# Quantised weights through DRAM with transposing loads, and other buffers and gather order ahead of the rounds

## What is computed

```python
xn = layernorm(x)
x = x + gnn(xn, edge_index) + mix(xn)          # graph attention, and linear attention without softmax
x = x + ffn(layernorm(x))

# gnn: rms-normalised x @ W_down, then xl = x @ Wl, xr = x @ Wr (4 heads of 64)
msg = xl[src] + xr[dst]
e = sum(leaky_relu(msg) * att);  p = exp(e - max_per_dst)
out = segment_sum(p / denom * xl[src]) @ W_up

# mix: q, k, v = projections of xn;  out = ((q k^T) * SCALE) v;  out @ Wo + bo

# ffn: every linear works on values rounded to 4-bit blocks of 16 with an 8-bit scale
gate = fq(x) @ fq(gate_w).T;  up = fq(x) @ fq(up_w).T
y = fq(silu(gate) * up) @ fq(down_w).T
```

## Time and profile before

| | us |
|---|---|
| median of three runs | 1021.11 |
| lowest and highest | 1013.91, 1021.95 |
| the profiled execution, in all | 1011.44 |
| its span | 1009.6 |
| mean granted PE clock in it | 0.954 of full |

### The profile page before, as it was taken

One profiled execution on the slowest core, in us unless ns is written; L12 is line 12 of the kernel. 1 busy time (PEld: TensorE's weight loads), 2 busy tenths in 40 slices (PEclk: granted clock), 3 DMA queues, 4 the chain that ended last, 5 costly groups with the idle time before them and its releaser, 6 DMA issues.

```text
span 1009.6 us, 9845 instructions
## 1 busy us (share of the span) xinstructions
PE 908.6 (90%) x2890; PEld 438.5 (43%) x2890; DVE 874.8 (87%) x1032; ACT 557.7 (55%) x1942; POOL 452.8 (45%) x502
## 2 busy tenths in 40 slices
PE   4999999999989999996998999979999779998655
PEld 3776454644344444442443444434444334443222
DVE  7997989976979999999988899788897698776996
ACT  2223133314787787778979898888793441222220
POOL 5210353215767777677776778777640000000000
PEclk9999999999979999998999999989999988999767
DMA  8204343524553533554335533338622000000012
GB/s 284 84 2 121 118 119 82 177 67 137 182 90 97 175 97 92 169 178 115 96 98 168 158 111 101 94 94 307 221 58 73 1 0 1 21 22 21 21 42 79
DMA packets 59460, 105.28 MB, mean 104 GB/s; under 512 B 24631, under 2 KB 32468, under 8 KB 59130
## 3 DMA queue, kind: packets, MB, share of 16 engines
q0 software_dynamic: 18560, 50.70, 19.0%
q1 hardware_dynamic: 40842, 53.92, 15.6%
HBM read 92.30 MB, written 12.45 MB: 104 GB/s over the span
## 4 chain that ended last, share of the span: by engine, by line
DVE 33%; PE 26%; ACT 23%; issue 14%; DMA 2%; POOL 1%; another core or an unknown queue 1%; DVEq 0%; ACTq 0%; POOLq 0%
ACT round_mem L1070 17%; PE acc L663 13%; PE acc L840 6%; DVE turned L1549 5%; DVE acc_sb L1416 5%; DVE z L1551 5%; DVE turned L1408 3%; ACT pz L1057 3%; PE acc L843 2%; DVE round_mem L1169 1%; PE acc L873 1%; PE turned L891 1%; DVE round_mem L1170 1%; DVE round_mem L1168 1%
## 5 line engine op out<-in xcount | busy, mean ns | idle before, releaser
L507 POOL DMA_INDIRECT round_mem<-msg_table,idx x352 | 337.0, 957 | 177.1 <-issue 79.3
L1070 ACT ACTIVATE round_mem<-round_mem,pz 128x65 f32<-128x65 f32 x1408 | 361.6, 398 | 49.0 <-issue 28.1
L663 PE MATMUL acc<-wslot,big_a 128*128 128x512 f32 x512 | 227.9, 606 | 13.1 <-remote 7.5
L663 PEld LDWEIGHTS acc<-wslot,big_a 128*128 128x128 f32 x512 | 98.8, 195 | 138.2 <-issue 129.8
L1416 DVE TENSOR_REDUCE acc_sb<-round_mem 128x260 f32<-128x1820 f32 (+1 forms) x62 | 121.6, 1961 | 42.9 <-ACT round_mem L1070 20.7
L663 PE MATMUL acc<-big_b,wslot 128*128 128x512 f32 x256 | 112.6, 602 | 6.2 <-remote 6.2
L663 PE MATMUL acc<-wslot,big_b 128*128 128x512 f32 x256 | 110.0, 592 | 0.0
L1408 DVE TENSOR_TENSOR turned<-round_mem,turned 128x1560 f32<-128x1560 f32 (+1 forms) x62 | 105.4, 1700 | 4.8 <-issue 2.0
L1551 DVE TENSOR_REDUCE z<-turned 128x24 f32<-128x1560 f32 (+1 forms) x62 | 105.1, 1695 | 2.1
L1549 DVE SCALAR_TENSOR_TENSOR turned<-turned,att_sb 128x1536 f32<-128x1536 f32 (+1 forms) x62 | 103.5, 1670 | 0.0
L1057 ACT ACTIVATE pz<-z 128x7 f32<-128x7 f32 (+1 forms) x248 | 56.8, 295 | 55.2 <-issue 40.6
(11 more groups left out here) (201 smaller groups left out, 1058.6 us busy)
## 6 DMA issues: line engine op xcount, KB each, us to landing
big_b<-in_x SPq DMA_DIRECT2D x18, 512.0 KB
round_mem<-msg_table,idx POOLq DMA_INDIRECT x352
out_x<-big_b SPq DMA_DIRECT2D x9, 512.0 KB
wslot<-in_wv_t SPq DMA_DIRECT2D x2, 2048.0 KB
wslot<-in_wk_t SPq DMA_DIRECT2D x2, 2048.0 KB
wslot<-in_wo_t SPq DMA_DIRECT2D x2, 2048.0 KB
wslot<-in_wq SPq DMA_DIRECT2D x2, 2048.0 KB
wslot<-in_gate_w SPq DMA_DIRECT2D x1, 2048.0 KB
```

The source lines that it names most:

```text
L507: pool.indirect_dma_start(xg[g % 4][:, j, :], None, msg_table, bass.IndirectOffsetOnAxis(idx[:, c, j0 + j:j0 + j + 1], 0)).then_inc(xg_in[ ...
L663: mm = nc.tensor.matmul(o(acc[:, n % 4, :]), a, b, start=first, stop=last)
L1070: ins = nc.scalar.activation(to[:, :, j], xg[g % 4][:, j, h * HR + 1:(h + 1) * HR], ACT.Copy, scale=pz[:, g % 2, j, h:h + 1])
```

## The change

- The stored layout is the natural one: `gu_dram` is (1024, 1024) and `dn_dram` (1024, 512), in bf16. SP writes VectorE's rounded piece itself, as soon as `wq_done` says it is there. `turn_weights`, ScalarE's `piece`, `TURNED_AFTER`, `wq_tp` and `wq_taken` are gone. The loads ahead of the feed-forward part become twelve DMAs with `transpose=True`, one per 128 columns.
- VectorE's piece q waits for the write of piece q-2 (`wt_out`) where it waited for `wq_tp`.
- The rounded pieces lie where the stage buffers were, `wt` at column 3168 (in xg[2]), `blk_max[0]` in the last 256 columns of xg[1], a third `blk_max` in `acc_sb` (so the third `weight_max` waits for `table_out`). Gather 1 goes ahead of the wait for the last pieces; gather 2 waits for `wq_done` 12, gather 3 for `colsum_done`.
- POOL does a one-column tensor_tensor on `tick` after gather 0, ahead of reading the flag.
- VectorE's body for extra rounds has two multiplications where it had R + 1 = 7, per chunk. VectorE's wait for `wq_taken` 12 is gone.
- The plan's constants change, and the 1 us added for groups with turns goes.

```diff
-PRODUCTS_AT, GROUP_STEP = 192.0, {"p0c": 2.0}
-ROUND_0_AT, ROUND_STEP = 232.0, 8.0
+PRODUCTS_AT, GROUP_STEP = 183.0, {"p0c": 2.0}
+ROUND_0_AT, ROUND_STEP = 229.0, 8.1
...
-        gu_dram = nc.dram_tensor("gu_dram", (P, KB, D), BF16, kind="Internal").ap()
-        dn_dram = nc.dram_tensor("dn_dram", (P, 4, D), BF16, kind="Internal").ap()
+        gu_dram = nc.dram_tensor("gu_dram", (2 * I, D), BF16, kind="Internal").ap()
+        dn_dram = nc.dram_tensor("dn_dram", (D, I), BF16, kind="Internal").ap()
...
-        behind = (R + 1) * ROW
-        wt = xg_mem[:, behind:behind + D]
-        wq_bf = [xg_mem[:, behind + D + i * I:behind + D + (i + 1) * I].bitcast(BF16) for i in range(2)]
-        wt_stage = [prod_mem[:, i * I:(i + 1) * I].bitcast(BF16) for i in range(2)]
-        blk_max = [xg_mem[:, behind + 2 * D:behind + 2 * D + 256], blk_max_1]
+        wt = xg_mem[:, 2 * R * ROW:2 * R * ROW + D]
+        wq_bf = [prod_mem[:, i * I:(i + 1) * I].bitcast(BF16) for i in range(2)]
+        blk_max = [xg_mem[:, 2 * R * ROW - 256:2 * R * ROW], blk_max_1, acc_sb[:, C - 1, 0:256]]
...
-                sp.wait_ge(wq_taken, q + 1)
-                st = wt_stage[q % 2]
+                sp.wait_ge(wq_done, q + 1)
                 if q < 8:
-                    sp.dma_start(gu_dram[:, :, q * P:(q + 1) * P], st.rearrange("p (k o) -> p k o", k=KB)).then_inc(wt_out[q % 2], 16)
+                    sp.dma_start(gu_dram[q * P:(q + 1) * P, :], wq_bf[q % 2]).then_inc(wt_out[q % 2], 16)
                 else:
                     d = q - 8
-                    sp.dma_start(dn_dram[:, :, d * 2 * P:(d + 1) * 2 * P],
-                                 st.rearrange("p (k o) -> p k o", k=4)).then_inc(wt_out[q % 2], 16)
+                    sp.dma_start(dn_dram[d * 2 * P:(d + 1) * 2 * P, :].rearrange("(j p) k -> p j k", p=P),
+                                 wq_bf[q % 2].rearrange("p (j k) -> p j k", j=2)).then_inc(wt_out[q % 2], 16)
...
-            sp.dma_start(wdn_sb, dn_dram).then_inc(tail_w_in, 16)
-            sp.dma_start(wgu_sb, gu_dram).then_inc(tail_w_in, 16)
+            for k in range(4):
+                sp.dma_start(wdn_sb[:, k, :], dn_dram[:, k * P:(k + 1) * P], transpose=True).then_inc(tail_w_in, 16)
+            for k in range(KB):
+                sp.dma_start(wgu_sb[:, k, :], gu_dram[:, k * P:(k + 1) * P], transpose=True).then_inc(tail_w_in, 16)
...
             gather(0)
+            nc.gpsimd.tensor_tensor(tick[:, 0:1], tick[:, 0:1], tick[:, 0:1], ALU.mult)
             rounds_over = pool.value_load(flags_i[0:1, 1:2], min_val=0, max_val=E)
             with pool.If(rounds_over > 0):
-                pool.wait_ge(wq_tp, 12)
+                pool.wait_ge(wq_done, 12)
...
-            pool.wait_ge(wq_tp, 12)
-            pool.wait_ge(colsum_done, 1)
             for g in range(1, LAST + 1):
+                if g == 2:
+                    pool.wait_ge(wq_done, 12)
+                if g == 3:
+                    pool.wait_ge(colsum_done, 1)
                 gather(g)
...
-                    pe.wait_ge(tail_w_in, 48)
+                    pe.wait_ge(tail_w_in, 16 * (4 + KB + 1))
...
-        early = {index_of["p", 0]: 203.0, index_of["p", 1]: 213.0, index_of["p", 2]: 214.0}
+        early = {index_of["p", 0]: 202.0, index_of["p", 1]: 212.0, index_of["p", 2]: 213.0}
...
-            if (kind, i) in TURNED_AFTER:
-                at += 1.0
...
+                if n == 2:
+                    dve.wait_ge(table_out, 16)
+                step(block_max(blk_max[n][:, :], wslot[n % 2][:, :]))
...
                 if q >= 2:
-                    dve.wait_ge(wq_tp, q - 1)
+                    dve.wait_ge(wt_out[q % 2], 16 * (q // 2))
...
-            dve.wait_ge(wq_taken, 12)
             rounds_over = dve.value_load(flags_i[0:1, 1:2], min_val=0, max_val=E)
...
-                        for j in range(R + 1):
-                            to = xg_over[:, j, :].rearrange("p (h d) -> p h d", d=HR)[:, :, 1:HR]
-                            of = to if j < R else running[c].rearrange("p (h d) -> p h d", d=MR)
-                            ins = nc.vector.tensor_tensor(to, of, pz[:, 0, j, :].unsqueeze(2).to_broadcast([NC, H, MR]), ALU.mult)
-                            if j >= R - 1:
-                                link(ins, r)
+                        to = xg_over.rearrange("p j (h d) -> p j h d", d=HR)[:, :, :, 1:HR]
+                        link(nc.vector.tensor_tensor(to[:, 0:R], to[:, 0:R], pz[:, 0, 0:R, :].unsqueeze(3).to_broadcast([NC, R, H, MR]), ALU.mult), r)
+                        link(nc.vector.tensor_tensor(to[:, R], running[c].rearrange("p (h d) -> p h d", d=MR),
+                                                     pz[:, 0, R, :].unsqueeze(2).to_broadcast([NC, H, MR]), ALU.mult), r)
```

More of the change, by code:

```diff
@@ L698, in _ @@
                         count_receivers(q)
-            def turn_weights(first, last):
-                for q in range(first, last):
-                    pe.wait_ge(wq_done, q + 1)
-                    if q >= 2:
-                        pe.wait_ge(wq_taken, q - 1)
-                    for k in range(KB):
-                        mm = nc.tensor.transpose(tpb[:, q % 2, k * P:(k + 1) * P], wq_bf[q % 2][:, k * P:(k + 1) * P], identb[:])
-                    mm.then_inc(wq_tp, 1)
             for c in range(C):
@@ L724, in _ @@
                              for c in range(C) for k in range(2)])
-            def turn_due(kind, i):
-                for q in TURNED_AFTER.get((kind, i), ()):
-                    turn_weights(q, q + 1)
             def sum_places():
@@ L1037, in _ @@
                         act.wait_ge(colsum2_done, 2 * (i - 3) + h + 1)
-            for i in range(16):
-                for q in TURNED_AFTER.get(("p", i), ()):
-                    piece(q)
             act.wait_ge(order_done, 2)
@@ L1309, in _ @@
             with dve.If(unordered > 0):
-                dve.wait_ge(wq_tp, 4)
+                dve.wait_ge(wt_out[0], 16 * 2)
+                dve.wait_ge(wt_out[1], 16 * 2)
                 dve.nop().then_inc(sort_count, 1)
```

33 lines of the change are left out of this document (5 added, 28 removed).

## The result

| | median us | ratio to the kernel before, 95% interval |
|---|---|---|
| kernel after, first chip | 1002.81 (1000.98 to 1006.45) | 0.9847 [0.9816, 0.9878] |
| kernel before beside it | 1020.17 | |
| repeat on a second chip | 969.77 | 0.9887 [0.9872, 0.9902] |
| repeat on a third chip | 970.45 | 0.9886 [0.9870, 0.9902] |

The account below looks back on a forecast made before the run. No one engine bounds throughout; the chain of waits does, mainly in VectorE's timeline at the head and end of the rounds. Terms -1.8 - 2.3 - 0.7 - 1.0 + 1.3 - 4.0 = -8.5 us gave 1012.6 us, range 1001 to 1027.

Parts of the forecast that it names:

- step 3: GpSimd in the head: either edit alone hides its pause at the first rescale, -2.3 us; a gather wait goes too, -0.7.
- step 5: Hand plan in the rounds: base takes move earlier, more ScalarE copies fall inside the rounds, +1.3 us (0 to 2).
- step 6: Last sum to first residual: base products end sooner and VectorE's waits go, -4.0 us; nothing in the tail is touched.
- Steps 1 and 2: Head: transposes and copies go, p starts sooner, -1.8 us for round 0; VectorE's new waits for piece writes cost nothing.
- Step 4: Gap behind VectorE's branch in the head: shorter skipped body and earlier place before the load's traffic, -1.0 us (0 to -3.7).
- Step 7: Twelve transposing loads ahead of the feed-forward part: start about 664, a few microseconds each, hidden in 82 us of cover, 0.
- The slow loads: Rival, ahead of the residual passes: transposing loads of T us each add 12 x (T - 6.8) us; chance 0.16.
- the late write: Rival, quantising: a write lands late behind its load, VectorE waits 3 to 8 us at a piece, 1013 to 1021; chance 0.04.
- The lead is eaten: Rival, rounds: ScalarE's pauses depend on absolute time, rounds end unmoved, only -4 us stays, 1017; chance 0.2.
- More comes off: Rival: branch gap closes by 3 us more and ScalarE's pauses shrink, -12 to -15 us, 1007; chance 0.2.

Follow-up runs that it names:

- the pieces' path alone: Kernel after with the plan constants of before, no one-column GpSimd operation, and gather 1 behind the twelfth piece: 1012.79 us, 0.9992 to the kernel before.
- the late load: Kernel after with the load of the second wv_t half issued behind the first logits: 997.18 us, 0.9835; on the third chip 971.51 us.
- the former plan: Kernel after with the plan constants of the kernel before: 974.78 us, 0.9941 on the quiet chip; 973.85 us, 0.9917 on the third.
- new plan: Kernel before with only the plan constants of the kernel after, without the 1 us for turns: 980.72 us, 0.9993.
- tick: Kernel before with only the one-column tensor_tensor added on GpSimd after gather 0: 1009.44 us, 0.9967.
- the one with the loads in pairs: Kernel of the late load with w_up and x loaded first and the twelve transposing loads in pairs, a pair a round: 968.48 us, 0.9869.
- the mixed plan: Kernel after with the former plan's rounds for p, p0, kv, t1 and t2, the new plan's for bias and base: 1007.09 us, 0.9934.

## Why the prediction was wrong

The mechanisms were named rightly for most steps; the sum fell short by 3 us on the quiet chips. Where, the traces say. The forecast's -0.7 for a gather comes behind round 3 and is counted in the second row; the third chip has no trace of the kernel before, so the quiet chip's stands in for it.

| stretch, us after less before | forecast | quiet chip | third chip | first chip |
|---|---|---|---|---|
| to the logits of round 3 (steps 1 to 4) | -5.1 | -6.9 | -6.2 | -7.6 |
| from there to the last sum (0.7 of step 3, step 5) | +0.6 | -0.5 | +0.3 | +9.1 |
| last sum to first residual (step 6) | -4.0 | -4.5 | -4.5 | -4.1 |
| first residual to the end (step 6) | 0 | -1.7 | -1.5 | -2.3 |
| in all, profiled executions | -8.5 | -13.6 | -11.9 | -4.9 |
| in all, medians | -8.5 | -11.8 | -11.0 | -17.4 |

**What failed.** Three terms were mis-sized. Step 6 has "Nothing in the tail is touched": a term put at nothing, which measured 1.5 to 2.3 us. Steps 5 and 6 price the hand plan in two parts that belong together, net 2.7 us; measured it is 3.7 and 3.2 at the first residual, and 5.0 and 3.4 by medians. And step 3 counts only the first two of VectorE's waits for GpSimd, while those in the later rounds shrank too. For the first chip the account stops short: its pair of traces shows 4.9 us of the 15.6 to 17.4, and what makes its medians differ by more is not known.

- **Steps 1 and 2, right.** p starts at 186.11 (186.3 forecast), both VectorE waits are gone, no piece waits for its write. The quantising ends 1.4 us sooner, not 0.5, but 0.8 of that is there at 83 us, where a load lands sooner, and in the traces of the changed kernels this end scatters from 220.4 to 223.5: no more than 0.5 is to be put down to the change.
- **Step 3, right in mechanism, too small.** The pause is hidden by either edit. Its price up to round 3 is 5.3 us, not 3.0, once VectorE's own lead of 3 to 5 us is there. With the pause left in, as in the pieces' path alone, that lead is gone at round 3. The step's "change of the kind of GpSimd operation costs 6 to 8 us" was too general: the pause comes once.
- **Step 4, a right sum in the wrong place.** The 6.2 us behind the branch stayed; the 2.53 us further on went, by the shorter body. Of this, as of the late load's 2.5 us, TensorE's p groups take part back at round 4.
- **Step 5, mis-sized.** I charged the plan 1.3 us in the rounds, 2 at most. Inside the changed kernel it costs 3.6 us on the quiet chip and 4.8 on the third up to the last sum, 0.5 and 0.8 of which are there when the quantising ends. The bound left out the p take a round too early.
- **Step 6, its other half.** I set the gain at the 4.0 us of waits that the earlier trace rows show. Measured from kernel before to kernel after that is nearly so, 25.4 to 20.9 us on the quiet chip. But against the former plan it is 7.3 us (8.0 on the third chip), since what is gained ahead would have been added to the base wait. The parts of the change other than the plan, forecast at 5.8, gave 6.8 and 7.6.
- **In the rounds** from round 4's logits to the last sum the quiet chip shows 462.2 us before, 460.5 after and 459.7 with the former plan, of which VectorE's waits for gathers and rescales are 6.1, 4.9 and 4.1: some 2 us that no step of the forecast has. That they shrank because GpSimd is ahead is my reading; no run takes it apart.
- **Step 7, near enough.** The twelve loads began at 672.7 (664 forecast) and were issued in 20.3 us, 1.7 us each; their small packets end between 696 and 698 us, some 24 us after the first issue, far inside the cover. By the Trainium skill (VectorE: DVE Perf Modes, The three transpose paths), 1,309 ns a block was an estimate of 126 us; the trace does not agree. By another page of the Trainium skill (DMA: Bandwidth & Descriptors, Latency and other measured facts), 261 GB/s, given there for a non-contiguous middle dimension, was an estimate of 12 us; measured are 3.1 MB in some 24 us, about 130 GB/s, with the gathers beside them. A cost of up to 3 us in the rounds stays possible.
- **Rivals.** The slow loads and the late write did not happen. "The lead is eaten" is what the first chip's single trace looks like (last sum 1.5 us late), and not what the medians and the quiet pairs say. "More comes off" names a size, 12 to 15 us, that the quiet chips nearly reach and the first passes, but by luck: neither of its reasons came true. The branch gap did not close, and ScalarE's pauses did not shrink (47.1 and 52.2 us ahead of its multiplications).
- **What stays open.** Four kernels with the whole change or nearly so have ratios of 0.9835 to 0.9847 on chips with ScalarE's pauses, and three have 0.9886 to 0.9889 without them; the intervals touch. Whether the change is worth more there is not shown.
- **The clock in the tail.** In the last 15 us the profiled kernel after has a granted clock of 0.82 and before of 0.64, means of TensorE's two levels (1.2 and 2.4 GHz); from the tenth residual to the end it is 85.1 and 86.9 us. All eighteen traces have one of these two lengths. The four of kernels without the new data path (before, its repeat, new plan, tick) are all at 86.8 to 86.9. On the quiet chips the four changed kernels with the new plan are at 85.0 to 85.1 and the two with the former plan at 86.8; on the others three changed kernels have the short one, one of them with the former plan, and five the long one. So the 1.7 us that the tail gave on the quiet chip lie here and go with the clock. Whether they are the change's is not shown, nor what decides the clock.

The clock in the windows of the last microseconds (window, us, busy of PE, PEld, DVE, ACT and POOL, clock, DMA share, GB/s), kernel after and before:

```profile
989.60:1004.60 15.00, 5.48 (x20) 1.98 (x20) 9.13 (x19) 0.59 (x1) 0.00 (x0) 0.82 0.26 97
```

```profile
994.50:1009.50 15.00, 7.75 (x20) 2.40 (x20) 7.68 (x11) 0.59 (x1) 0.00 (x0) 0.64 0.27 98
```

No kernel run here is shown to beat the kernel after; the one with the loads in pairs comes nearest.

## What to carry to other kernels

Price an edit against the kernel in which all the others are done: a wait is worth what it has grown to when its neighbours are gone, and three parts of this change (the plan, the pieces' path, the tick) measured 0.1, 0.1 and 0.3% singly, the first two not to be told from nothing, while the whole is worth over 1%. When a stretch gets shorter, ask which engine was only just in time at its end, and pull its work forward with its whole chain of inputs; half of the chain, as in the mixed plan, lost 8 us. Look for an idle stretch in which an engine can pay a fixed pause, and put one cheap operation of the coming kind there.

## What the runs showed of the hardware

- GpSimd pauses 6.9 to 7.7 us once in each of the eighteen traces, at its first tensor_tensor behind a run of gathers, wherever that is put.
- VectorE's pause behind a branch over a long body is 5.7 to 6.4 us from the branch's end, 3.4 to 3.7 with no 2 MB load beside it (three traces). A body 50 instructions longer adds a second pause of 2.1 to 3.1 us behind the next two instructions, 2.3 us on.
- The same kernel takes 982 us on two chips and 1013 to 1020 on three others. On the first and the quiet chip round 0's logits are done at the same time (240.9 and 241.0), and the whole difference comes in the rounds. The slower chips show pauses of ScalarE there, and fewer of VectorE (8 to 24 us in all), with nothing waited for or "remote"; the two quick ones show none between 240 and 760 us. Over 260 to 760 us, the group of ScalarE's multiplications (busy, mean ns, idle and its releasers), kernel before on the first chip and on the quiet one:

```profile
L1070 ACT ACTIVATE round_mem<-round_mem,pz 128x65 f32<-128x65 f32 x1344 | 345.7, 399 | 47.1 <-issue 28.1 <-remote 12.5 <-DVE acc_sb L1416 2.1
```

```profile
L1070 ACT ACTIVATE round_mem<-round_mem,pz 128x65 f32<-128x65 f32 x1353 | 340.6, 398 | 12.5 <-DVE acc_sb L1416 8.6
```

The kernel after has 52.2 and 10.2 us there. The change did not touch them, and no run shows what they wait for.
